# First layer's next-batch convolution as diagonal matmuls on TensorE, and one stash store issued a row later

## The chip, the cores and the metric

The kernel runs on one core of a Trainium2 chip. The metric is device microseconds (us) of one execution, as the median of several runs. PE is TensorE, DVE is VectorE, ACT is ScalarE, POOL is GpSimd, SP is SyncE, which here only issues DMAs.

## The reference, cut to what matters

The program is a stack of four layers over x (4 batches of 512 rows, 512 columns), each an "xattn" block and an "ffn" block. The change touches only the first block of layer 0, a selective state-space block on the context (4 batches of 512 positions, 256 columns, widened to 512 channels, 16 states):

```python
x = jnp.einsum('bld,ed->bel', hidden_states, in_proj_w)
xc = jax.lax.conv_general_dilated(x, conv_w, window_strides=(1,), padding=[(d_conv - 1, 0)],
                                  feature_group_count=d_inner, dimension_numbers=('NCH', 'OIH', 'NCH'))
x = silu(xc + conv_b[None, :, None])
x_dbl = jnp.einsum('bdl,ed->bel', x, x_proj_w)
dt = jax.nn.softplus(jnp.einsum('brl,dr->bdl', dt_low, dt_proj_w) + dt_proj_b[None, :, None])
A = -jnp.exp(A_log)
def step(state, inp):
    d, b, c, u = inp
    state = state * jnp.exp(d[..., None] * A) + (d * u)[..., None] * b[:, None, :]
    return state, jnp.einsum('bdn,bn->bd', state, c)
y = (y + D[None, :, None] * x) * silu(z)
```

The convolution is depthwise: each of the 512 channels has four taps along the sequence. Layer 2 has a block of the same form. Its input projection, convolution, silu and softplus ("the second mixer" below) are also computed inside this first stage, and kept in DRAM for later.

## The kernel before, in words

Channels lie on the 128 partitions in four groups e = 0 to 3, the 512 positions along the free axis; a 128x2048 operand holds all four groups. The first stage (`mamba(0)`) loops over the four batches, and in a batch over the 16 states n. The order of the work on every engine is written out by hand in the `body` of each engine's part; engines meet at semaphores.

In one state, VectorE multiplies (L1850) and scans along the sequence (L1852) all four channel groups. It may start the multiply of state n only when TensorE has turned state n-2 (the last transposes of L1282) and the row of B for state n has come from DRAM (SyncE, L498), and the scan only when ScalarE has made the decay exp(delta*A) (L871, called `decay(n)` and made at ScalarE's place n-2). TensorE transposes the state (L1282, `turn_h`), ScalarE evicts it with a scale (L857, `take_h`), TensorE adds it up, turned back, in PSUM (L1293, `add_h`).

Between these, each engine has other work at fixed places:

- The front of a mixer is: input projection on TensorE (`inproj`), eviction into `m_pad` (ScalarE, L806), convolution (`convolve`, VectorE, L1807 and L1809: 4 multiplies and 12 multiply-adds of 128x512), silu (ScalarE, L813), x projection (TensorE, L1239), dt projection (TensorE; L839 and L840 evict it on ScalarE), `exp_abs` (ScalarE, L846), `softplus` (VectorE, L1821, L1822, L1825), `ln_w` (ScalarE, L850).
- Mixer 1, the second mixer for this batch, runs its convolution after VectorE's state 2, its dt in states 3 and 4, `exp_abs` at the end of ScalarE's place 5, and `softplus` after VectorE's state 6.
- Mixer 0 of the next batch has its input projection in TensorE's state 2, its convolution on VectorE after state 6 (ahead of mixer 1's softplus), silu in ScalarE's place 6, x projection in TensorE's state 6, dt in 7 and 8, softplus after VectorE's state 10. The last batch has none of it.
- Twelve units of keys and values for a later stage (`keys_values`, 16 instructions of 128x256 on TensorE, two evictions at L881, two stores and a weight load issued by GpSimd) stand in the states that `KV_ORDER` lists; the last batch has the first eight.
- PSUM banks 4 to 7 rotate over all tiles in the order of `mamba_tiles`: a tile waits until the tile four before it is evicted (`free`).
- SyncE issues in order. Around state 9: row 8, the store of D*u (1 MB, L511, which waits for ScalarE's L931 of place 7), row 9, a small store, row 10, a load of the context (L501, which waits for the eighth unit of keys and values, made in TensorE's state 9), row 11.

ScalarE's tables: Silu, Exp and Ln need different ones here, and an ACT_TABLE_LOAD stands wherever the next function needs another one; Copy, Abs and Relu run between them without one.

Of the kernel before, what the change touches and what calls it, by code (L numbers as in the profile page):

```python
# [14 lines left out]
P = 128  # L15
# [24 lines left out]
KV_ORDER = (4, 5, 6, 6, 7, 8, 8, 9, 10, 11, 12, 13)  # L40
# [10 lines left out]
def mamba_tiles(last):  # L51
# [4 lines left out]
    for n in range(DS):  # L56
# [15 lines left out]
        if n == 6 and not last:  # L72
            names += [("x", 0)]
        if n in (7, 8) and not last:
            names += [("dt", 0, 2 * (n - 7) + e) for e in range(2)]
# [59 lines left out]
def flamingo(nc, x_d, ctx_d, small_d, rows_d, min_d, mdt_d, ffn_d, qk_d, head_d, wo_d, bit_d, out_d, stages=STAGES):  # L135
    with ExitStack() as stack:
# [83 lines left out]
        pad3 = t3(m_pad, NE)  # L220

# [233 lines left out]
        def _(sp):  # L455
# [10 lines left out]
            for b in range(B):  # L466
                if b == 3:
                    at, n = ROWS["b1"]
                    sp.dma_start(p_b1, rows_d[:, at:at + n].partition_broadcast(P)).then_inc(b1_raw, 16)
# [8 lines left out]
            def mamba(stage):  # L478
# [13 lines left out]
                def body(b, last):  # L492
                    tile = batch_tiles(b, last)
                    for n in range(DS):
# [9 lines left out]
                        if n == 5:  # L504
                            store_bc(1, b, tile("x", 1)[0])
                        if n == 9 and not last:
                            store_bc(0, b + 1, tile("x", 0)[0])
                        if n == 8:
# [155 lines left out]
        def _(pool):  # L664
# [80 lines left out]

            for i in range(KV_LEAD):
# [23 lines left out]
        def _(act):  # L770
# [25 lines left out]
            def mamba(stage):  # L796
# [3 lines left out]
                def take_inproj(m, f, tile):  # L800
                    if not (isinstance(f, int) and f == 0):
                        act.wait_ge(conv_done, 2 * f)
                    for e in range(NE):
                        i, bank = tile("in", m, e)
                        act.wait_ge(tile_filled, i + 1)
                        nc.scalar.activation(pad3[:, e, DC - 1:], ps[:, bank, :], ACT.Copy).then_inc(tile_taken, 1)  # L806

# [75 lines left out]
                def body(b, last):  # L883
                    front_b, front_a = 2 * b + 1, 2 * b + 2
                    tile = batch_tiles(b, last)
                    for n in range(DS):
# [9 lines left out]
                        if n == 8 and not last:  # L896
                            act.wait_ge(sp_corrected, front_b + 1)
                        if n in (8, 9) and not last:
                            take_dt(0, n - 8, tile)
# [21 lines left out]
                        if n == 6 and not last:  # L921
                            silu_u(front_a, 0)
                        if late is not None:
                            take_kv(late, b * (KV_HEADS * 16) + (KV_LEAD + late) * 16, tile)
                        if n == 6:
                            ln_w(front_b)
                            if not last:
                                take_xd(front_a, 0, b + 1, tile)
# [5 lines left out]
                        if n == 9 and not last:  # L934
                            exp_abs(0, tile)
                        if n == 10:
                            if not last:
                                ln_w(front_a)
# [260 lines left out]
        def _(pe):  # L1199
# [16 lines left out]
            def mamba(stage):  # L1216
# [24 lines left out]

                def turn_c(tile):
# [54 lines left out]
                def body(b, last):  # L1297
                    tile = batch_tiles(b, last)
                    for n in range(DS):
# [30 lines left out]
                        if n == 6 and not last:  # L1330
                            xproj(2 * b + 2, 0, tile)
                        if n in (7, 8) and not last:
                            dt(0, n - 7, tile)
# [20 lines left out]
                pe.wait_ge(diag_ready, 1)  # L1354
                batches(pe, body)
# [347 lines left out]
        def _(dve):  # L1703
# [93 lines left out]
            def mamba(stage):  # L1797
# [56 lines left out]
                def body(b, last):  # L1854
                    front_b, front_a = 2 * b + 1, 2 * b + 2
                    tile = batch_tiles(b, last)
                    for n in range(2, DS):
# [9 lines left out]
                        if n == 6:  # L1867
                            if not last:
# [546 lines left out]
```

## Time and profile before

| | |
|---|---|
| median of 3 runs | 3713.45 us (3708.44 to 3716.21) |
| the profiled execution | 3708.7 us, its span 3707.1 us |
| busy share over the span | PE 93%, DVE 81%, ACT 47%, POOL 17% |
| busy share of DVE, first stage (0 to 735 us) | 651.39 of 735 us |
| busy share of PE, first stage | 615.25 of 735 us |
| granted PE clock, mean | 0.966 |

The first stage is the first 730 us. One batch in it is 170.7 us long, from one state 2 to the next. A row of the timeline gives start, duration, engine, line, what is written and read, and how many instructions were merged into the row; in brackets the idle time before it and who ended it. The line numbers are those of the kernel before.

### The profile page before, as it was taken

Reading aid. Unit: us, or ns where it says so; the run is one execution under the profiler, and the core shown is the slowest. Engines: PE = TensorE matmul, PEld = TensorE weight load, DVE = VectorE, ACT = ScalarE, POOL = GpSimd, SP = SyncE. Lnnn points to the kernel's source line nnn. Section 1 sums busy time; section 2 is a strip of 40 time slices with the busy share of each in tenths; the row PEclk is TensorE's granted clock in tenths of the full one; section 3 lists DMA queues with packets and bytes.
Section 4 is the critical chain, followed back from the end, with each engine's and each line's share of the span. In section 5 each row is a group of like instructions: output and inputs, shape, how many; then the busy total and the mean of one; then the engine's idle time right before and its main releaser. Section 6 shows DMA issues by size and latency. Waiting matters only on the chain.

```text
span 3707.1 us, 40267 instructions
## 1 busy us (share of the span) xinstructions
PE 3437.8 (93%) x12305; PEld 1947.9 (53%) x12322; DVE 3013.5 (81%) x4951; ACT 1759.9 (47%) x2748; POOL 623.9 (17%) x596
## 2 busy tenths in 40 slices
PE   7888888799999999899999899999999999999887
PEld 4667676544444444444445788655455455455443
DVE  8899998797979798789889867688388388388797
ACT  6878787633333223334443311255155155155297
POOL 2324251243433220134331000000000000000000
PEclk9899988999999999999999999999999999999998
DMA  4324241524342322443444300221021022021000
GB/s 156 133 65 148 66 147 59 196 86 147 102 153 93 137 84 92 156 153 97 149 156 175 145 24 23 104 70 60 31 70 60 21 70 70 20 70 64 32 12 34
DMA packets 91260, 345.73 MB, mean 93 GB/s; under 512 B 11841, under 2 KB 20161, under 8 KB 77793
## 3 DMA queue, kind: packets, MB, share of 16 engines
q1 hardware_dynamic: 61552, 226.90, 17.4%
q0 software_dynamic: 29552, 116.94, 9.6%
q8 instruction: 76, 1.25, 0.1%
q14 instruction: 80, 0.65, 0.1%
HBM read 280.88 MB, written 62.91 MB: 93 GB/s over the span
## 4 chain that ended last, share of the span: by engine, by line
PE 48%; DVE 27%; issue 14%; ACT 6%; DMA 3%; DVEq 0%; POOL 0%; ACTq 0%; POOLq 0%; SPq 0%
PE ps L1213 30%; PE ps L1610 6%; PE ps L1600 3%; DVE room L1782 3%; PE ps L1441 2%; DVE room L1786 2%; DMA room<-bc_scratch 2%; DVE room L1790 2%; PE ps L1493 2%; PE ps L1282 2%; DVE room L1852 1%; DVE room L1795 1%; DVE room L1850 1%; ACT room L871 1%; DVE room L2320 1%
## 5 line engine op out<-in xcount | busy, mean ns | idle before, releaser
L1213 PE MATMUL ps<-lnT,room 128*128 128x512 f32 x2240 | 987.0, 596 | 23.1 <-DVE room L2007 16.0
L1213 PEld LDWEIGHTS ps<-lnT,room 128*128 128x128 f32 x2240 | 426.0, 191 | 567.9 <-issue 525.5
L1213 PE MATMUL ps<-room 128*128 128x512 f32 (+2 forms) x1807 | 666.8, 524 | 49.6 <-ACT room L1138 21.1
L680 POOL TENSOR_TENSOR idle<-idle 128x1 f32<-128x1 f32 x268 | 447.1, 1668 | 1263.4 <-ACT room L881 434.6
L1213 PEld LDWEIGHTS ps<-room 128*128 128x128 f32 (+1 forms) x1824 | 289.9, 163 | 404.5 <-issue 258.4
L1441 PE MATMUL ps<-room 128*128 128x512 f32 x864 | 379.7, 597 | 8.5 <-DVE room L1961 8.5
L792 ACT ACTIVATE room<-room,small 128x511 f32<-128x511 f32 x256 | 163.6, 710 | 380.6 <-DVE room L1786 380.5
L1852 DVE TENSOR_TENSOR_SCAN room<-room 128x2048 f32<-128x2048 f32 x64 | 283.2, 4425 | 19.0 <-ACT room L871 13.8
L1786 DVE TENSOR_TENSOR_SCAN room<-room 128x2048 f32<-128x2048 f32 x64 | 283.4, 4428 | 5.9 <-DVE room L1782 0.9
L1441 PEld LDWEIGHTS ps<-room 128*128 128x128 f32 x864 | 165.1, 192 | 215.2 <-issue 208.3
L1112 ACT ACTIVATE room<-ps,stat 128x512 f32<-128x512 f32 x256 | 199.0, 777 | 137.3 <-DVE stat L2268 137.3
L1282 PE MATMUL ps<-ident,room 128*128 128x128 f32 x1088 | 164.9, 310 | 86.1 <-DVE room L1852 47.0
L1610 PE MATMUL ps<-room 128*128 128x512 f32 x512 | 242.2, 597 | 0.0
L1768 DVE SCALAR_TENSOR_TENSOR xres<-ps,gates,xres 128x512 f32<-128x512 f32 (+1 forms) x64 | 45.7, 747 | 234.8 <-PE ps L1213 179.9
L2267 DVE TENSOR_REDUCE stat<-ps 128x1 f32<-128x512 f32 x256 | 177.0, 691 | 67.4 <-PE ps L1213 67.1
L1282 PEld LDWEIGHTS ps<-ident,room 128*128 128x128 f32 x1088 | 142.1, 160 | 116.6 <-DVE room L1852 50.3
L1213 PE MATMUL ps<-x,w 128*128 128x512 f32 x768 | 180.2, 395 | 9.2 <-DVE mw L2073 8.2
L1782 DVE TENSOR_TENSOR room<-room 128x2048 f32<-128x2048 f32 x64 | 146.3, 2286 | 40.4 <-DMA room<-bc_scratch 38.7
L857 ACT ACTIVATE room<-ps,room 128x512 f32<-128x512 f32 x256 | 157.1, 699 | 27.8 <-PE ps L1282 27.1
L1213 PEld LDWEIGHTS ps<-x,w 128*128 128x128 f32 x768 | 145.5, 190 | 42.3 <-DVE mw L2073 9.4
L871 ACT ACTIVATE room<-room,small 128x511 f32<-128x511 f32 x256 | 164.5, 739 | 0.5 <-DVE room L1831 0.3
L1850 DVE TENSOR_TENSOR room<-room 128x2048 f32<-128x2048 f32 x64 | 145.8, 2278 | 19.6 <-DMA room<-bc_scratch 18.4
(284 smaller groups left out, 5105.1 us busy)
## 6 DMA issues: line engine op xcount, KB each, us to landing
room<-in_ffn SPq DMA_DIRECT2D x16, 2048.0 KB, 10.9
room<-bc_scratch POOLq DMA_DIRECT2D x128, 256.0 KB, 3.6
room<-kv_stash SPq DMA_DIRECT2D x64, 512.0 KB, 3.4
kv_stash<-room POOLq DMA_DIRECT2D x96, 256.0 KB, 2.4
room<-stash POOLq DMA_DIRECT2D x24, 1024.0 KB, 5.2
room<-in_ffn SPq DMA_DIRECT2D x20, 1024.0 KB, 5.1
room<-in_ffn SPq DMA_DIRECT2D x24, 768.0 KB, 5.6
room<-in_ffn SPq DMA_DIRECT2D x12, 1536.0 KB, 7.3
```

What stands on the lines that cost most here:

```text
L680: nc.gpsimd.tensor_tensor(idle[:, :], idle[:, :], idle[:, :], ALU.add).then_inc(zeros_added, 1)
L871: last_a = nc.scalar.activation(t3(m_dA[n % 2], NE)[:, e, 1:], delta3[:, e, 1:], ACT.Exp, scale=alog[:, e, n:n + 1])
L1112: nc.scalar.activation(P3[:, t, :], ps[:, 4 + t, :], ACT.Exp, bias=nb[:, t:t + 1], scale=rs[:, t:t + 1], accum_out=total[:, t:t + 1]).then ...
L1213: last = nc.tensor.matmul(out, lhsT, rhs, start=(i == 0), stop=(i == len(parts) - 1))
L1282: mm = nc.tensor.transpose(ps[:, bank, e * P:(e + 1) * P], a3[:, e, t * P:(t + 1) * P], ident[:, :])
L1441: mm = nc.tensor.matmul(ps[:, t, :], hT[:, j, t * P:(t + 1) * P], w[:, j, :], start=(g == 0 and j == 0), stop=(g == 3 and j == n - 1))
L1610: mm = nc.tensor.matmul(ps[:, 0, :], kv[:, k, HD:2 * HD], PT3[:, k, :], start=(k == 0), stop=(k == NT - 1))
L1782: v.tensor_tensor(h3, t3(s_du, NE), Bn, ALU.mult).then_inc(s_dBu_ready, 1)
L1786: v.tensor_tensor_scan(s_h, s_dA, s_h, 0.0, ALU.mult, ALU.add).then_inc(s_scan_done, 1)
L1850: link(v.tensor_tensor(t3(h, NE), t3(m_du, NE), Bn, ALU.mult))
L1852: v.tensor_tensor_scan(h, m_dA[n % 2], h, 0.0, ALU.mult, ALU.add).then_inc(scan_done, 1)
L2267: link(v.tensor_reduce(mx[:, t:t + 1], ps[:, 4 + t, :], AX.X, ALU.max, negate=True))
```

## The change

1. `KV_ORDER` becomes (1, 4, 5, 6, 7, 8, 8, ...): one of the two units of state 6 goes, and all that precede it move up, so that the first stands in state 1.
2. Mixer 0's convolution for the next batch is no longer on VectorE. GpSimd makes 16 diagonal matrices (4 taps by 4 groups, 128x128) once, at the start, in the place in `xres` of the last batch's x. In states 3, 4, 5 and 6 TensorE convolves one group each as four matmuls with the shifted `m_pad`, into a rotating PSUM tile. ScalarE takes the tile with Silu and bias (`silu_conv`) at its places 4 to 7, ahead of the state's `take_h`. After the odd groups TensorE waits for its own tile.
3. What follows moves one state on: x projection to state 7, dt to 8 and 9, evictions of dt to ScalarE's places 9 and 10, softplus to VectorE's state 11, `ln_w` to place 11.
4. SyncE issues the store of D*u behind row 9 and the small store instead of ahead of row 9. It waits for x's last batch no longer at the start: that load is issued in the last batch's state 1.

The first batch's own convolution, before the loop, and all of mixer 1's stay on VectorE.

```diff
-KV_ORDER = (4, 5, 6, 6, 7, 8, 8, 9, 10, 11, 12, 13)
+KV_ORDER = (1, 4, 5, 6, 7, 8, 8, 9, 10, 11, 12, 13)
...
+        if n in (3, 4, 5, 6) and not last:
+            names += [("conv", n - 3)]
...
+        m_taps = xres[:, (B - 1) * NT * D:].rearrange("p (j e n) -> p j e n", j=DC, e=NE)
...
                         if n == 9 and not last:
                             store_bc(0, b + 1, tile("x", 0)[0])
-                        if n == 8:
+                        if n == 9:
+
                             place = stashed(2, b)
                             sp.wait_ge(Du_ready, b + 1)
                             sp.dma_start(place, m_z).then_inc(Du_stored, 16)
...
+            for j in range(DC):
+                for e in range(NE):
+                    ins = nc.gpsimd.tensor_scalar(m_taps[:, j, e, :], ident[:, :], t3(const(("cw", 0)), NE)[:, e, j:j + 1], None,
+                                                  ALU.mult)
+                ins.then_inc(taps_ready, 1)
...
+                def silu_conv(f, e, tile):
+
+                    u3, cb = t3(m_next[0][0], NE), const(("cb", 0))
+                    i, bank = tile("conv", e)
+                    act.wait_ge(tile_filled, i + 1)
+                    ins = nc.scalar.activation(u3[:, e, :], ps[:, bank, :], ACT.Silu, bias=cb[:, e:e + 1])
+                    ins.then_inc(tile_taken, 1)
...
+                def convolve(e, tile):
+                    pe.wait_ge(tile_taken, tile("in", 0, e)[0] + 1)
+                    i, bank = tile("conv", e)
+                    free(i)
+                    mm = product(ps[:, bank, :], [(m_taps[:, j, e, :], pad3[:, e, j:j + S]) for j in range(DC)])
+                    mm.then_inc(tile_filled, 1)
+                    if e % 2:
+                        pe.wait_ge(tile_filled, i + 1)
+                        pe.sem_inc(conv_done, 1)
...
                         if n == 6:
-                            if not last:
-                                dve.wait_ge(Du_summed, b + 1)
-                                convolve(front_a, 0, tile)
                             softplus(front_b, 1)
...
-                        if n == 10 and not last:
+                        if n == 11 and not last:
                             softplus(front_a, 0)
```

VectorE behind state 6, before: the end of the convolution (L1809) and then mixer 1's softplus (L1821 to L1825).

```order
L1807 TENSOR_SCALAR room<-room,small 128x512
L427 REGISTER_ALU
L1809 SCALAR_TENSOR_TENSOR room<-room,small 128x512 x2
...
L1820 ISA
L1821 TENSOR_SCALAR room<-room 128x2048
L427 REGISTER_ALU
L1822 SCALAR_TENSOR_TENSOR room<-room 128x2048
```

The same place now: the scan of state 6 (L1898) and the softplus (L1867 on) right behind it.

```order
L1896 TENSOR_TENSOR room<-room 128x2048
L432 REGISTER_ALU
L1897 REGISTER_ALU
L1898 SCALAR_TENSOR_TENSOR room<-room 128x2048
L1866 ISA
L1867 TENSOR_SCALAR room<-room 128x2048
```

All 16 instructions of the convolution are gone from between the two. ScalarE's place 5, before: from the last eviction of dt (L840) to `exp_abs` (L846).

```order
L840 ACTIVATE room<-ps,small 128x512
L856 REGISTER_ALU
L857 ACTIVATE room<-ps,room 128x512 [waits tile_filled]
...
L871 ACTIVATE room<-room,small 128x511 x4
L879 REGISTER_ALU
L880 REGISTER_ALU [waits kv_stored0]
L881 ACTIVATE room<-ps 128x512 [waits tile_filled]
L880 REGISTER_ALU [waits kv_stored1]
L881 ACTIVATE room<-ps 128x512 [waits tile_filled]
L846 ACTIVATE room<-room 128x2048 [waits tile_taken]
```

The same place now (L871 evicts dt, L833 is the new Silu, L888 `take_h`, L902 the decay, L912 keys and values, L877 `exp_abs`).

```order
L871 ACTIVATE room<-ps,small 128x512
L832 REGISTER_ALU
L833 ACT_TABLE_LOAD
L833 ACTIVATE room<-ps,small 128x512 [waits tile_filled]
L887 REGISTER_ALU [waits tile_taken]
L888 ACTIVATE room<-ps,room 128x512 [waits tile_filled]
...
L902 ACT_TABLE_LOAD
L902 ACTIVATE room<-room,small 128x511 x4
...
L877 ACTIVATE room<-room 128x2048 [waits tile_taken]
```

A Silu and two table loads now stand ahead of `exp_abs` in place 5, and the same three in place 4. SyncE from row 9 to row 11, before (L498 the rows, L511 the store of D*u, L501 the context).

```order
L511 ISA [waits Du_ready]
L511 DMA stash<-room 128x2048
L497 REGISTER_ALU
L498 ISA [waits scan_done]
L498 DMA room<-bc_scratch 128x512
L482 REGISTER_ALU
L483 ISA [waits tile_taken]
L483 DMA bc_scratch<-room 32x512
```

The same place now (L509 the rows, L525 the store, L512 the context).

```order
L509 DMA room<-bc_scratch 128x512
L493 REGISTER_ALU
L494 ISA [waits tile_taken]
L494 DMA bc_scratch<-room 32x512
L525 ISA [waits Du_ready]
L525 DMA stash<-room 128x2048
...
L512 ISA [waits tile_filled]
L512 DMA room<-in_ctx 128x1024
L508 REGISTER_ALU
L509 ISA [waits scan_done]
L509 DMA room<-bc_scratch 128x512
```

The store stands behind row 9 now; the load of the context still stands ahead of row 11.

## Rows read from the trace of the kernel before

**Rows 1.** Busy time by stretch: each engine (instructions), granted clock, DMA share, GB/s.

```profile
230.00:401.00 171.00, 147.93 (x798) 114.24 (x798) 158.21 (x103) 134.58 (x210) 57.09 (x60) 0.91 0.32 105
```

**Rows 2.** VectorE's timeline, second batch: start, us, engine, line, what, [idle before].

```profile
231.35 2.28 DVE L1850 TENSOR_TENSOR room<-room 128x2048 f32<-128x2048 f32 x1
...
278.34 0.86 DVE L1807 TENSOR_SCALAR room<-room,small 128x512 f32<-128x512 f32 x2
...
288.60 1.22 DVE L1821 TENSOR_SCALAR room<-room 128x2048 f32<-128x2048 f32 x1
...
294.39 2.28 DVE L1850 TENSOR_TENSOR room<-room 128x2048 f32<-128x2048 f32 x1
...
319.91 2.29 DVE L1850 TENSOR_TENSOR room<-room 128x2048 f32<-128x2048 f32 x1 [4.69 <-DMA room<-bc_scratch]
...
339.75 1.23 DVE L1821 TENSOR_SCALAR room<-room 128x2048 f32<-128x2048 f32 x1 [1.75 <-ACT room L846]
...
345.54 2.28 DVE L1850 TENSOR_TENSOR room<-room 128x2048 f32<-128x2048 f32 x1
...
402.09 2.29 DVE L1850 TENSOR_TENSOR room<-room 128x2048 f32<-128x2048 f32 x1
```

**Rows 3.** ScalarE's timeline, second batch.

```profile
285.88 1.98 ACT L846 ACTIVATE room<-room 128x2048 f32<-128x2048 f32 x1
...
292.40 1.17 ACT L881 ACTIVATE room<-ps 128x512 f32<-128x512 f32 x2
293.59 1.28 ACT L813 ACT_TABLE_LOAD   x1
294.89 2.56 ACT L813 ACTIVATE room<-room,small 128x512 f32<-128x512 f32 x4
```

**Rows 4.** VectorE's timeline, last batch, where there is no convolution of mixer 0.

```profile
572.64 2.28 DVE L1850 TENSOR_TENSOR room<-room 128x2048 f32<-128x2048 f32 x1
...
629.48 1.23 DVE L1821 TENSOR_SCALAR room<-room 128x2048 f32<-128x2048 f32 x1 [9.37 <-ACT room L846]
...
635.27 2.29 DVE L1850 TENSOR_TENSOR room<-room 128x2048 f32<-128x2048 f32 x1
...
660.60 2.29 DVE L1850 TENSOR_TENSOR room<-room 128x2048 f32<-128x2048 f32 x1 [4.60 <-DMA room<-bc_scratch]
```

**Rows 5.** TensorE's timeline, second batch; a 128x512 matmul is two of these instructions.

```profile
228.96 3.60 PE L1312 MATMUL ps<-room 128*128 128x512 f32 x8
232.40 1.91 PE L1293 MATMUL ps<-ident,room 128*128 128x128 f32 x16
...
247.19 2.39 PE L1293 MATMUL ps<-ident,room 128*128 128x128 f32 x16 [0.61 <-ACT room L857]
...
268.12 0.66 PE L1282 MATMUL ps<-ident,room 128*128 128x128 f32 x4 [1.42 <-ACT room L840]
269.28 0.98 PE L1282 MATMUL ps<-ident,room 128*128 128x128 f32 x4 [0.50 <-ACT room L840]
...
288.48 3.72 PE L1213 MATMUL ps<-down_rows,room 128*128 128x256 f32 x16 [0.31 <-ACT room L857]
...
325.51 1.98 PE L1213 MATMUL ps<-room,mw 16*128 16x512 f32 x4
...
333.01 4.27 PE L1213 MATMUL ps<-down_rows,room 128*128 128x256 f32 x16
```

**Rows 6.** SyncE's timeline, second batch.

```profile
313.20 0.36 SPq L511 DMA_DIRECT2D stash<-room  x1
313.81 0.33 SPq L498 DMA_DIRECT2D room<-bc_scratch  x1
...
338.05 0.33 SPq L498 DMA_DIRECT2D room<-bc_scratch  x1
```

**Rows 7.** DMA issues of line 498, same stretch.

```profile
DMA to landing us min/median/max: 3.3/3.8/9.1
```

**Rows 8.** GpSimd's timeline, the head.

```profile
18.20 0.35 POOL L680 TENSOR_TENSOR idle<-idle 128x1 f32<-128x1 f32 x1 [16.08 <-issue]
```

More of the change, by code:

```diff
@@ L71, in mamba_tiles @@
             names += [("dt", 1, 2 * (n - 3) + e) for e in range(2)]
-        if n == 6 and not last:
+        if n in (3, 4, 5, 6) and not last:
+            names += [("conv", n - 3)]
+        if n == 7 and not last:
             names += [("x", 0)]
-        if n in (7, 8) and not last:
-            names += [("dt", 0, 2 * (n - 7) + e) for e in range(2)]
+        if n in (8, 9) and not last:
+            names += [("dt", 0, 2 * (n - 8) + e) for e in range(2)]
         if n == 15 and not last:
@@ L895, in body @@
                             take_dt(1, n - 4, tile)
-                        if n == 8 and not last:
+                        if n == 9 and not last:
                             act.wait_ge(sp_corrected, front_b + 1)
-                        if n in (8, 9) and not last:
-                            take_dt(0, n - 8, tile)
+                        if n in (9, 10) and not last:
+                            take_dt(0, n - 9, tile)
+                        if n == 4 and not last:
+                            act.wait_ge(Du_summed, b + 1)
+                        if n in (4, 5, 6, 7) and not last:
+                            silu_conv(front_a, n - 4, tile)
                         if n:
@@ L926, in body @@
                             ln_w(front_b)
-                            if not last:
-                                take_xd(front_a, 0, b + 1, tile)
+                        if n == 7 and not last:
+                            take_xd(front_a, 0, b + 1, tile)
                         if n == 7:
@@ L1329, in body @@
                             dt(1, n - 3, tile)
-                        if n == 6 and not last:
+                        if n in (3, 4, 5, 6) and not last:
+                            convolve(n - 3, tile)
+                        if n == 7 and not last:
                             xproj(2 * b + 2, 0, tile)
-                        if n in (7, 8) and not last:
-                            dt(0, n - 7, tile)
+                        if n in (8, 9) and not last:
+                            dt(0, n - 8, tile)
                         if n == 15 and not last:
@@ L1879, in body @@
                             v.tensor_tensor(m_u2, m_nd2, m_u2, ALU.mult).then_inc(stash_ready, 1)
-                        if n == 10 and not last:
+                        if n == 11 and not last:
                             softplus(front_a, 0)
```

34 lines of the change are left out of this document (22 added, 12 removed).

## The prediction

> **What bounds the kernel now.** I read the busy time by stretch first. In a middle batch of the first stage VectorE is busy 158.21 of 171 us, TensorE 147.93, ScalarE 134.58 [rows 1]. So VectorE sets the pace by share, with about 13 us idle, but TensorE has only 23 us of room. A share does not tell what follows when work leaves VectorE, so I then read VectorE's timeline for the places where it waits and what ends the wait, then the other engines' timelines for who is nearly late there. A batch is 402.09 - 231.35 = 170.74 us [rows 2].
>
> The decisive pair of rows: mixer 1's softplus starts on VectorE at 288.60 [rows 2], and what it waits for, `exp_abs` on ScalarE, ran from 285.88 to 287.86 [rows 3]. Its input came 0.7 us before VectorE asked. The convolution that the change removes is what VectorE did meanwhile.
>
> **The convolution taken from VectorE.** From 278.34 to 288.60 it costs 10.26 us in each of three batches [rows 2], 30.8 us in all. Without it VectorE asks for the softplus at 278.34 and waits for ScalarE until 287.9, 9.5 us: 0.7 us of the 10.26 is left if nothing else moves. The trace has this case already. The last batch has no such convolution, and there VectorE waits 9.37 us for L846; from state 2 to state 7 it takes 635.27 - 572.64 = 62.63 us [rows 4] against 294.39 - 231.35 = 63.04 us with the convolution [rows 2].
>
> **What makes `exp_abs` later.** It stands at the end of ScalarE's place 5, so it follows TensorE's transposes of state 5, and these follow all TensorE work of states 1 to 4.
> - A matmul with a diagonal of the same shape exists (D*u): 4 of them are 8 instructions, from 228.96 to 232.40, 3.44 us [rows 5]. The new convolution puts 3.44 us into each of states 3 to 6.
> - State 3's 3.44 us stands in front of transposes that before waited 1.42 + 0.50 us for the evictions of dt [rows 5]. Those evictions now run beside it: 1.5 us is added. State 4's: 3.2 us, the waits there being short.
> - The unit of keys and values moved into state 1 is 16 instructions in 3.6 us (3.72 with the overlap of the last) [rows 5]. The 0.61 us wait in state 2 [rows 5] goes, and so does some 0.8 us by which ScalarE lagged there (an estimate): 2.1 us is left.
> - Together 6.8 us on TensorE. On ScalarE, two Silus (2.56/4 = 0.64 us each) and four table loads stand in places 4 and 5: 1.28 + 4 x 1.3 = 6.5 us [rows 3]. Beside TensorE's 6.8 us of delay they mostly fit. If only ScalarE's counted, the delay were about 3.5; if both came in series, about 10.3. I take 6.2, near TensorE's, since a Silu's load runs while its tile is made.
>
> So `exp_abs` ends at 287.9 + 6.2 = 294.1, the softplus starts 5.5 us later than before, and state 7 as well. The 10.26 us come back as a wait of about 15.7.
>
> A page of the Trainium skill would make this worse. In these rows a switch of tables costs 1.3 us: an eviction ends at 293.57, the load starts at 293.59, the Silu at 294.89 [rows 3]. "ScalarE: Activation LUTs", What ACT_TABLE_LOAD costs, gives about 1.28 us for the load and a drain of about 1.38 us besides. By that rule the four switches would put 5.5 us more ahead of `exp_abs` in a batch, some 16 us in all; the trace agrees with the load and shows no such drain, so I leave it out.
>
> **The store behind row 9.** VectorE waits 4.69 us for row 9 [rows 2], because SyncE sat in front of the store until D*u was ready at 313.20, and only then issued the row, at 313.81 [rows 6]. With the store behind it, row 9 goes out at the end of state 7's scan and lands (3.8 us) within the layernorm. This gives 4.69 us per batch and 4.60 in the last [rows 4]. State 9 stands at 5.5 - 4.7 = +0.8 us.
>
> **Row 11, a new wait.** Before, mixer 0's softplus stood behind state 10 and took, with its 1.75 us wait, from 338.00 to 345.54 [rows 2]. Row 11 was issued at 338.05 [rows 6], behind the load of the context, which waits for a unit of keys and values of TensorE's state 9 (from 333.01) [rows 5]. The softplus covered its 3.8 us flight [rows 7]. Now the softplus stands behind state 11, so VectorE wants row 11 at 338.0 + 0.8 = 338.8, while TensorE is late. Its balance up to that unit: 6.8, + 3.44 in state 5, + 3.44 - 3.6 - 3.44 in state 6 (one unit and the x projection gone, which is 8 instructions as a convolution is), + 3.44 - 1.98 in state 7 (dt gone to 8) [rows 5], about 8.1; some waits of TensorE in states 7 to 9 (4 to 5 us) absorb half. I take 4.3, bounds 2.5 and 8. Row 11 is issued at 342.4 and lands at 346.1: a wait of 7.3 us, and state 11 starts 0.5 us later than before. Then come its 6.75 us and the softplus with its wait, 7.5 us, which before lay ahead of it: state 12 and all later ones are +8. Since ScalarE's `exp_abs` of mixer 0 may run partly ahead, I take +7.3 a batch. TensorE's mean granted clock is 0.91 of the full 2.4 GHz in such a batch [rows 1]; I count no gain from denser work.
>
> **At no cost.** GpSimd's diagonals: 16 small operations at the start, where it was idle for 16.08 us ahead of its first store's 18.20 [rows 8]; with one 1 MB load fewer in the head against them, -2 to +4 us. The last x load: 1 MB in the last batch, needed at its state 8. TensorE's wait for its own tile: 0.3 us, inside the sums.
>
> **The sum.** Three batches at +7.3 = +21.9. The last batch: -4.6 for row 9, +2.1 because the moved unit delays its `exp_abs` too: -2.5. Head 0. So +19.4 us on the profiled execution's 3708.7 us (its span 3707.1 and 1.6 around it): 3728. The median of the runs is 4.8 us above that execution, which would give 3733; I say 3730. By bounds: with 3.5 us for `exp_abs` and row 11 hardly late, a batch is 0 and the total -3 to 0, 3706; with 10.3 and 8, a batch is +12, the total +34, and about 3750.
>
> **The rivals.**
> - Faster, "VectorE is the bound": all 10.26 and 4.69 us come off, 30.8 + 18.7 = 49 us, 3664. For it: VectorE's 93% share of a batch [rows 1]. Against it: the 9.37 us wait in the last batch. It needs `exp_abs` 9 us earlier, and nothing moves it up.
> - Slightly faster, "the wait takes the convolution's place exactly, the store pays": TensorE's and ScalarE's additions hide, row 11 comes in time. A batch is -0.7 - 4.7 = -5.4, total about -21, 3692. Against it: TensorE's waits ahead of state 5's transposes are 0.61, 1.42 and 0.50 us [rows 5], less than the 6.9 us of new matmuls there. It decides this way if `exp_abs` moves by less than 1 us.
> - No change: `exp_abs` moves by about 3.5 us and row 11 is late by 2 or 3: within 7 us of before.
> - Much slower, ScalarE in series: TensorE waits for ScalarE's evictions behind each new load, as rotating banks make it. +12 a batch, 3750. Counted in the order, ScalarE gets 7 more loads a batch (15 for 8), 9 us on 134.58 busy [rows 1].
> - That the convolution is not moved: excluded by the order of instructions.
>
> **How the numbers follow.** My forecast (+8 to +30 us) has 0.6, much slower 0.13, no change 0.14, slightly faster 0.09, fully faster 0.04. A measurement tells about 0.2% (7.4 us) from no change. So slower 0.74, same 0.14, faster 0.12. The range from 3700 to 3752 leaves out the fast rivals and the far end of the slow one, 2 in 10 at most.
>
> **What would show it.** Right: in a middle batch, VectorE waits 14 to 17 us for `exp_abs` behind state 6, row 9 without a wait, row 11 with 5 to 8 us, a batch of 176 to 180 us; the last batch 2 to 3 us shorter. Wrong at the first step: `exp_abs` within 1 us of 56.5 us after state 2's start. Wrong at row 11: no wait there, then the batch is near 171. The forecast fails as a whole if a batch is below 170 us.

## The result, and the profile after

| | before | after |
|---|---|---|
| median (shared chip) | 3712.81 us (3708.44 to 3716.21, 4 runs) | 3743.48 us (3740.68 to 3745.26, 4 runs) |
| profiled execution | 3708.7 us | 3742.7 us |
| middle batches of the first stage | 170.7, 170.6 us | 182.2, 184.0 us |
| last x row of the first stage starts at | 724.33 us | 755.51 us |

The ratio is 1.0083, 95% interval 1.0065 to 1.0100: slower, by 31 us. Of the 34 us between the profiled executions, 31.2 are there at the end of the first stage. Counted from state 2 to state 2 they are: head -0.2, the three batches with a convolution for the next one +9.9, +11.4 and +13.5, the last -2.0, its end -1.4. An offset below is the time since the start of a batch's state 2.

In the second batch VectorE is now busy 148.40 of 182.15 us, ScalarE 142.62, TensorE 158.61 [rows 1] at a higher granted clock (0.94 for 0.91). VectorE did lose its 10 us of work; the batch got 11 us longer.

```profile
241.07:423.22 182.15, 158.61 (x829) 117.28 (x828) 148.40 (x88) 142.62 (x215) 57.64 (x60) 0.94 0.31 99
```

VectorE's timeline of that batch, changed kernel (L1896 and L1898 are a state's multiply and scan, L1853 the convolution's first multiply, L1867 the softplus; state 2 starts at 241.07):

```profile
241.07 2.28 DVE L1896 TENSOR_TENSOR room<-room 128x2048 f32<-128x2048 f32 x1
...
249.89 0.49 DVE L1853 TENSOR_SCALAR room<-room,small 128x512 f32<-128x512 f32 x1 [1.23 <-ACT room L826]
...
275.58 2.29 DVE L1896 TENSOR_TENSOR room<-room 128x2048 f32<-128x2048 f32 x1 [2.23 <-PE ps L1325]
280.59 4.42 DVE L1898 TENSOR_TENSOR_SCAN room<-room 128x2048 f32<-128x2048 f32 x1 [2.72 <-ACT room L902]
...
291.06 4.42 DVE L1898 TENSOR_TENSOR_SCAN room<-room 128x2048 f32<-128x2048 f32 x1 [3.08 <-ACT room L902]
306.64 1.36 DVE L1867 TENSOR_SCALAR room<-room 128x2048 f32<-128x2048 f32 x1 [11.15 <-ACT room L877]
...
312.57 2.29 DVE L1896 TENSOR_TENSOR room<-room 128x2048 f32<-128x2048 f32 x1
...
333.24 2.28 DVE L1896 TENSOR_TENSOR room<-room 128x2048 f32<-128x2048 f32 x1
...
359.63 2.29 DVE L1896 TENSOR_TENSOR room<-room 128x2048 f32<-128x2048 f32 x1 [8.21 <-DMA room<-bc_scratch]
...
367.61 1.23 DVE L1867 TENSOR_SCALAR room<-room 128x2048 f32<-128x2048 f32 x1 [1.14 <-ACT room L877]
...
373.40 2.28 DVE L1896 TENSOR_TENSOR room<-room 128x2048 f32<-128x2048 f32 x1
```

State 12 of the kernel before, which [rows 2] leave out:

```profile
352.29 2.27 DVE L1850 TENSOR_TENSOR room<-room 128x2048 f32<-128x2048 f32 x1
```

Against it and [rows 2], as offsets: softplus of mixer 1 at 65.6 for 57.3 (it waits 11.15 us), state 7 at 71.5 for 63.0, state 9 at 92.2 for 88.6 and without a wait, state 11 at 118.6 for 114.2, behind a new wait of 8.21 us for its row, state 12 at 132.3 for 120.9.

ScalarE's timeline (L833 is the Silu out of the convolution's bank, L877 `exp_abs`, L912 the eviction of keys and values), then SyncE's (L525 the store of D*u, L512 the context, L509 rows):

```profile
294.48 1.28 ACT L833 ACT_TABLE_LOAD   x1
296.53 0.69 ACT L833 ACTIVATE room<-ps,small 128x512 f32<-128x512 f32 x1 [0.77 <-PE ps L1246]
...
304.71 1.90 ACT L877 ACTIVATE room<-room 128x2048 f32<-128x2048 f32 x1
...
344.69 0.60 ACT L912 ACTIVATE room<-ps 128x512 f32<-128x512 f32 x1 [4.39 <-DMA kv_stash<-room]
347.12 0.60 ACT L912 ACTIVATE room<-ps 128x512 f32<-128x512 f32 x1 [1.84 <-DMA kv_stash<-room]
```

```profile
334.77 0.35 SPq L525 DMA_DIRECT2D stash<-room  x1
...
354.98 0.35 SPq L512 DMA_DIRECT2D room<-in_ctx  x1
355.59 0.33 SPq L509 DMA_DIRECT2D room<-bc_scratch  x1
```

`exp_abs` starts 63.6 us after state 2, for 54.5 before [rows 3]. Row 11 is issued at 114.5, for 106.7 [rows 6].

### The profile page after: what moved, and what is told of

The parts are those of the page before. It is cut to its first block, busy times and chain, and to the rows that moved or that the text cites. A ratio compares the mean times of both kernels' runs of the same rounds, so it can differ in the third digit from the quotient of the medians.

```text
span 3741.0 us, 40462 instructions
## 1 busy us (share of the span) xinstructions
PE 3469.7 (93%) x12401; PEld 1954.1 (52%) x12418; DVE 2985.1 (80%) x4903; ACT 1786.5 (48%) x2769; POOL 655.8 (18%) x612
## 4 chain that ended last, share of the span: by engine, by line
PE 51%; DVE 25%; issue 13%; ACT 7%; DMA 3%; POOL 0%; DVEq 0%; ACTq 0%; POOLq 0%; SPq 0%
PE ps L1246 32%; PE ps L1656 5%; PE ps L1487 3%; PE ps L1646 3%; DVE room L1828 2%; DMA room<-bc_scratch 2%; PE ps L1539 2%; PE ps L1325 2%; DVE room L1832 2%; DVE room L1836 1%; DVE room L1898 1%; DVE room L1896 1%; ACT room L902 1%; ACT room L888 1%; PE ps L1336 1%
## 5 line engine op out<-in xcount | busy, mean ns | idle before, releaser
L1246 PE MATMUL ps<-lnT,room 128*128 128x512 f32 x2240 | 989.0, 598 | 25.3 <-DVE room L2052 18.7
L694 POOL TENSOR_TENSOR idle<-idle 128x1 f32<-128x1 f32 x268 | 466.4, 1740 | 1264.1 <-ACT room L912 463.1
L1898 DVE TENSOR_TENSOR_SCAN room<-room 128x2048 f32<-128x2048 f32 x64 | 283.2, 4425 | 29.5 <-ACT room L902 24.1
L2312 DVE TENSOR_REDUCE stat<-ps 128x1 f32<-128x512 f32 x256 | 176.9, 691 | 67.1 <-PE ps L1246 66.8
L1325 PE MATMUL ps<-ident,room 128*128 128x128 f32 x1088 | 154.4, 298 | 79.6 <-DVE room L1898 38.6
L1325 PEld LDWEIGHTS ps<-ident,room 128*128 128x128 f32 x1088 | 134.0, 154 | 112.9 <-DVE room L1898 44.6
L1896 DVE TENSOR_TENSOR room<-room 128x2048 f32<-128x2048 f32 x64 | 145.9, 2280 | 37.9 <-DMA room<-bc_scratch 27.2
L888 ACT ACTIVATE room<-ps,room 128x512 f32<-128x512 f32 x256 | 155.9, 693 | 25.0 <-PE ps L1325 24.3
L902 ACT ACTIVATE room<-room,small 128x511 f32<-128x511 f32 x256 | 164.0, 728 | 0.6 <-DVE room L1877 0.3
## 6 DMA issues: line engine op xcount, KB each, us to landing
room<-in_ffn SPq DMA_DIRECT2D x16, 2048.0 KB, 10.8
```

Source lines behind the costliest of these rows:

```text
L694: nc.gpsimd.tensor_tensor(idle[:, :], idle[:, :], idle[:, :], ALU.add).then_inc(zeros_added, 1)
L888: nc.scalar.activation(hT3[:, t, :], ps[:, bank, :], ACT.Copy, scale=cT3[:, t, column:column + 1]).then_inc(tile_taken, 1)
L902: last_a = nc.scalar.activation(t3(m_dA[n % 2], NE)[:, e, 1:], delta3[:, e, 1:], ACT.Exp, scale=alog[:, e, n:n + 1])
L1246: last = nc.tensor.matmul(out, lhsT, rhs, start=(i == 0), stop=(i == len(parts) - 1))
L1325: mm = nc.tensor.transpose(ps[:, bank, e * P:(e + 1) * P], a3[:, e, t * P:(t + 1) * P], ident[:, :])
L1896: link(v.tensor_tensor(t3(h, NE), t3(m_du, NE), Bn, ALU.mult))
```

## The experiments

Every row but "after" (the result's four runs) is timed in five rounds against the kernel before on the same chip (its medians there: 3711.2, 3710.8 and 3709.7 us). "Batches" are the two middle ones, "stage" the start of the last x row, both from VectorE's timeline of the profiled execution. That is one execution, and executions of one kernel lie up to 21 us apart (3700.5 to 3721.3 for the kernel before), so a few us between two stages tell little by themselves.

| kernel | median us | ratio to before, 95% | batches | stage |
|---|---|---|---|---|
| before | 3711.2 | 1 | 170.7, 170.6 | 724.3 |
| b_store: + store behind row 9 | 3702.7 | 0.9975 (0.9962 to 0.9988) | 167.5, 169.4 | 710.3 |
| b_kv: + new order of keys and values | 3717.5 | 1.0012 (1.0000 to 1.0025) | 177.4, 176.9 | 736.2 |
| b_conv: + convolution on TensorE | 3768.5 | 1.0156 (1.0135 to 1.0178) | 191.9, 191.3 | 783.8 |
| after: all three | 3743.5 | 1.0083 (1.0065 to 1.0100) | 182.2, 184.0 | 755.5 |
| a_store8: after, without the store's move | 3748.3 | 1.0096 (1.0078 to 1.0115) | 184.3, 186.4 | 763.4 |
| a_oldkv: after, without the new order | 3753.7 | 1.0110 (1.0092 to 1.0127) | 188.9, 187.3 | 771.2 |
| a_kctx: after, context's load in place 13 | 3761.1 | 1.0134 (1.0114 to 1.0154) | 189.4, 187.8 | 775.0 |
| a_kctx11: the same, behind row 11 | 3748.4 | 1.0098 (1.0080 to 1.0115) | 183.7, 184.6 | 759.0 |
| a_tap1: after, one tap of four | 3743.5 | 1.0085 (1.0067 to 1.0104) | 183.5, 178.6 | 751.6 |
| a_copy: after, Relu for Silu | 3726.6 | 1.0043 (1.0027 to 1.0059) | 177.2, 179.6 | 744.0 |
| a_group: after, Silus together | 3738.2 | 1.0078 (1.0059 to 1.0098) | 182.6, 182.3 | 755.3 |
| b_late0: b_store, softplus and context's load one place later | 3706.0 | 0.9990 (0.9979 to 1.0001) | 173.8, 173.1 | 726.2 |
| b_both: b_late0, last batch's softplus behind state 7 | 3712.5 | 1.0005 (0.9992 to 1.0018) | 173.7, 174.0 | 728.2 |

**The parts alone.** The store:

```diff
-                        if n == 8:
+                        if n == 9:
                             place = stashed(2, b)
```

> The kernel before with one edit: the store of D*u stands behind row 9 on SyncE instead of ahead of it (place 9 for place 8). Theory A (what sets a batch is the way over TensorE and ScalarE, VectorE's waits are partly a shadow of it): VectorE's wait of 4.69 us for row 9 goes, of which about two thirds stay as a gain at the batch's end, since TensorE and ScalarE are then nearer to late in states 9 to 13: 4 x 3 = 12 us, about 3701. Theory B (the prediction's own term, each wait counted where it stands): 3 x 4.69 + 4.60 = 18.7 us, about 3694. Theory C (the store pays nothing, the wait comes back at the next state): 3713.

Row 9's wait is gone, and the kernel is 8.5 us faster by the medians (14 us at the stage's end of the profiled execution, which lies 10.8 us under this kernel's median). Neither sum is the 18.7 us of waits removed: some came back one place later, at mixer 0's softplus, 4.23 us for 1.75 [rows 2]. Theory A is the nearest.

```profile
310.21 2.28 DVE L1850 TENSOR_TENSOR room<-room 128x2048 f32<-128x2048 f32 x1
...
332.53 1.35 DVE L1821 TENSOR_SCALAR room<-room 128x2048 f32<-128x2048 f32 x1 [4.23 <-ACT room L846]
```

The order of keys and values:

```diff
-KV_ORDER = (4, 5, 6, 6, 7, 8, 8, 9, 10, 11, 12, 13)
+KV_ORDER = (1, 4, 5, 6, 7, 8, 8, 9, 10, 11, 12, 13)
```

> The kernel before with one edit: the new order of the units of keys and values (one moved from state 6 to state 1). Theory A: 16 instructions of 3.6 us stand ahead of state 5's transposes, so mixer 1's exp_abs is about 2 us later; before, it was ready 0.7 us ahead of VectorE behind the convolution, so 1.4 us in each of three batches and 2.1 in the last come through: +6, about 3719. Theory B (the unit fills time in which TensorE waited anyway): within 2 us of 3713. Theory C (exp_abs is later by the full 3.6 us): 3 x 2.9 + 3.6 = +12, about 3725.

The median says +6.3, as theory A did. The middle batches are 6.3 to 6.7 us longer, and the place is another than A's: VectorE waits 4.2 us for the first evictions of the input projection ahead of mixer 1's convolution, where before there was no wait. The moved unit does not stand ahead of those projections; an idle stretch of TensorE does, told at the end. Without it they would be 2.5 and 1.9 us longer, and `exp_abs`, 6.6 us later in the second batch, is 2.4 later beyond it. The first batch has no such stretch ahead of it: `exp_abs` is 1.1 us later there, and the batch is as long as before (171.78 for 171.77). So most of this run's time is the idle stretch and not theory A's term, and A's number came out by luck.

The convolution alone is the changed kernel with both other edits undone:

> The third part of the change alone: the kernel before with the convolution on TensorE in states 3 to 6 and what moves with it, but with the old order of keys and values and the store of D*u ahead of row 9. Theory I (parts add as each measured in the changed kernel: the store gives back about 5 us there, the new order of keys and values about 10): about 3759. Theory J (parts add as each measured in the kernel before: store -8.5, order of keys and values +6, so the convolution is the change's +31 less these): +33, about 3744. Theory K (the prediction's sum for the convolution alone, its row 11 and exp_abs terms without store and without the moved unit): about +30, 3741.

It costs 59 us, more than any theory had. A middle batch is 21 us longer, and 13 of these are a longer wait for row 9. VectorE's, ScalarE's and SyncE's timelines of its third batch (state 2 at 443.82; L854 is the eviction of the x projection, L964 is D*u):

```profile
551.26 2.29 DVE L1896 TENSOR_TENSOR room<-room 128x2048 f32<-128x2048 f32 x1 [17.70 <-DMA room<-bc_scratch]
```

```profile
522.02 0.60 ACT L912 ACTIVATE room<-ps 128x512 f32<-128x512 f32 x1 [6.02 <-DMA kv_stash<-room]
524.27 0.60 ACT L912 ACTIVATE room<-ps 128x512 f32<-128x512 f32 x1 [1.65 <-DMA kv_stash<-room]
...
541.28 0.59 ACT L854 ACTIVATE room<-ps 48x512 f32<-48x512 f32 x1 [3.76 <-PE ps L1272]
541.78 2.55 ACT L964 ACTIVATE room<-room,small 128x512 f32<-128x512 f32 x4
```

```profile
544.50 0.36 SPq L525 DMA_DIRECT2D stash<-room  x1
545.12 0.33 SPq L509 DMA_DIRECT2D room<-bc_scratch  x1
```

Row 9 stands behind the store, the store behind ScalarE's D*u, and that behind two units of keys and values in state 6: the second unit's eviction waits 6.0 us until GpSimd's store of the first has left its buffer. D*u's store goes out 100.7 us after state 2, for 81.9 before [rows 6]. Some 7 of these 19 us belong to the second unit: with one unit in state 6, in the changed kernel, the store goes out at 93.7 (334.77 above). The rest is `exp_abs`, itself late, and the eviction of the x projection, which now stands ahead of D*u and waits 3.76 us for TensorE.

A good part of the 6.0 us is not the store. Ahead of each store GpSimd runs a tiny addition on a tile of its own (L694), and the store is issued only when that is done. GpSimd's timeline, then VectorE's beside it:

```profile
504.74 0.19 POOL L694 TENSOR_TENSOR idle<-idle 128x1 f32<-128x1 f32 x1 [7.26 <-ACT room L912]
...
515.68 3.96 POOL L694 TENSOR_TENSOR idle<-idle 128x1 f32<-128x1 f32 x1 [8.48 <-ACT room L912]
519.58 0.56 POOL L703 DMA_DIRECT2D kv_stash<-room  x1
```

```profile
515.23 4.42 DVE L1898 TENSOR_TENSOR_SCAN room<-room 128x2048 f32<-128x2048 f32 x1
```

At 504.74 VectorE stood idle, waiting for `exp_abs`, and the addition took 0.19 us. At 515.68 it ran beside a scan, took 3.96 us, and ended with the scan (519.64 and 519.65). The eviction started 2.4 us after the store's issue. No run takes this addition away.

So the change's two smaller parts repair what its first part does, and each is worth more beside the convolution than in the kernel before: the store's move 15 us (b_conv to a_oldkv), the new order 20 us (b_conv to a_store8), together 25.

**The parts taken back from the changed kernel.**

> The changed kernel with one edit: the store of D*u stands ahead of row 9 again. Theory A: row 9 is late by about 5 us again and most of it comes through, +3 to +5 us per batch and in the last: +14, about 3757; row 11's wait gets shorter by what state 9 starts later. Theory B (the store's move gives its full 4.69 us four times): +19, about 3762. Theory C (in the changed kernel VectorE would only wait at row 11 instead, whose row depends on TensorE and not on VectorE): row 11's wait falls from 8 to 4 us, the time stays within 4 us of 3743.

Between A and C: 4.8 us. VectorE waits 8.23 us for row 9 again, and row 11's wait falls from 8.21 to 1.53 us. One wait stands for the other.

> The changed kernel with the old order of the units of keys and values (state 1 has none, state 6 has two). In the kernel before, the new order alone cost 12 us up to the end of the stage, 4.2 us of it in each batch as VectorE's wait for the input projection ahead of mixer 1's convolution. Theory A (the way TensorE to ScalarE sets the batch): that wait (1.6 to 3.5 us here) goes and state 7 starts 2 to 4 us earlier, but the unit now stands in state 6 in front of mixer 0's exp_abs, and some of it is paid there: -5, about 3739. Theory B (the parts of the change add up): -6 to -12, about 3735. Theory D (TensorE alone is the bound, and its idle time in state 1 is lost): 3.6 us more per batch, +11, about 3754.

Theory D's number, 3754, but not shown for its reason: as in b_conv, the second unit of state 6 waits for GpSimd's store of the first (7.04 us in the second batch, 3.82 of them GpSimd's addition beside a scan).

**Row 11.**

```diff
-                        if n == 10 and not last:
+                        if n == 13 and not last:
                             sp.wait_ge(tile_filled, tile("kv", KV_OWN - 1, 1)[0] + 1)
```

> The changed kernel with one edit: SyncE's load of the context, which stood ahead of row 11 (place 10) and waits for a unit of keys and values, is issued in place 13. Theory B (the prediction's own term: row 11's wait of 7.3 us, measured 8.2 to 10.2, adds to the path because the row sits behind this load): that wait goes and comes off in three batches, 3 x 8 = 24 to 27 us, about 3718. Theory A (TensorE and ScalarE are what is late there): row 11 comes in time, but VectorE then waits some 7 to 8 us more for mixer 0's exp_abs behind state 11 (it waited 0.3 to 1.1 us there): within 4 us of 3743.

Row 11's wait went, and the time rose by 18 us. The 1 MB store of state 11, no longer behind the context's load, went out at 349.24, 103.9 us after state 2 for 115.1 in the changed kernel. A store of keys and values, issued beside it at 349.06, landed late: ScalarE waited 4.91 us for it (1.84 in the changed kernel):

```profile
349.24 0.36 SPq L529 DMA_DIRECT2D stash<-room  x1
```

```profile
354.60 0.60 ACT L912 ACTIVATE room<-ps 128x512 f32<-128x512 f32 x1 [4.91 <-DMA kv_stash<-room]
```

So the load was put behind row 11 but ahead of that store (`n == 11`):

> The changed kernel with the context's load on SyncE right behind row 11 instead of ahead of it, and still ahead of the 1 MB store of state 11 (with the load in place 13, that store went out 6.9 us earlier, a store of keys and values landed later, and the time was 17 us longer). Theory A (TensorE to ScalarE set the batch, row 11 is a shadow): row 11 in time, but the wait for mixer 0's exp_abs takes its place: within 4 us of 3743. Theory B (row 11's wait of 8.2 to 10.2 us is on the path): -24, about 3719. Theory H (an earlier state 11 brings VectorE's waits and the 1 MB store forward and costs as in the run with place 13): about 3760.

Row 11 is now in time, and nothing is won (+5 us by the medians, with overlapping intervals). VectorE's timeline, state 11 and behind it:

```profile
352.55 2.27 DVE L1896 TENSOR_TENSOR room<-room 128x2048 f32<-128x2048 f32 x1
356.01 4.42 DVE L1898 TENSOR_TENSOR_SCAN room<-room 128x2048 f32<-128x2048 f32 x1 [1.20 <-ACT room L902]
370.96 1.23 DVE L1867 TENSOR_SCALAR room<-room 128x2048 f32<-128x2048 f32 x1 [10.53 <-ACT room L877]
```

The 8.21 us at row 11 have become 10.53 at the softplus. Theory B, the prediction's own term as a cause, is dead: the wait was real, but taking it away only moves it. The run also fits the reading of a_kctx: with the 1 MB store back behind the load, ScalarE's wait is 1.81 us again.

**TensorE or ScalarE.** One tap (three of the four are left out):

```diff
-[(m_taps[:, j, e, :], pad3[:, e, j:j + S]) for j in range(DC)]
+[(m_taps[:, j, e, :], pad3[:, e, j:j + S]) for j in range(1)]
```

> The changed kernel, but each tile of the convolution on TensorE is made of one tap of four (three taps are left out, so it computes something else): 2 matmul instructions for 8, some 2.6 us less in each of states 3 to 6, 10.3 us a batch; ScalarE's work and all loads of tables stay. Theory A (TensorE's added matmuls delay exp_abs): exp_abs of mixer 1 comes about 4 us earlier (63.6 to about 59 us after state 2), that of mixer 0 about 7 us earlier: -7 in each of three batches, -21, about 3722. Theory E (ScalarE's Silus and table loads are what delays it): within 4 us of 3743. Theory F (both the TensorE term and the wait at row 11): -10 per batch, about 3713.

Some 10 us a batch less of matmuls at full clock change nothing in the median (the profiled execution is 7 us shorter, the batches differ by 5 us from each other). Theory A, that TensorE's added matmuls are what costs, fell here as far as this run can tell. In TensorE's timeline the room became waits for ScalarE, and after them a unit of keys and values ran at 6.00 us for 3.72 [rows 5]:

```profile
283.70 1.11 PE L1325 MATMUL ps<-ident,room 128*128 128x128 f32 x4 [1.34 <-ACT room L833]
284.61 6.00 PE L1246 MATMUL ps<-down_rows,room 128*128 128x256 f32 x16
...
309.16 0.66 PE L1325 MATMUL ps<-ident,room 128*128 128x128 f32 x4 [2.73 <-ACT room L833]
```

The granted clock is 0.60 in those 6.00 us, for 1.00 in the same unit of the changed kernel. Over the whole batch it is 0.91 for 0.94, and TensorE is busy only 2.0 us less than in the changed kernel (156.65 for 158.61), not 10:

```profile
239.88:423.35 183.47, 156.65 (x811) 118.39 (x810) 148.45 (x88) 143.35 (x217) 57.23 (x60) 0.91 0.29 98
```

So in this batch the run tests less than its edit promises: most of what was left out came back as slower matmuls. The first batch is the cleaner test. There TensorE is busy 7.0 us less (148.28 for 155.23), yet `exp_abs` comes no earlier (62.4 for 62.0) and the batch is 1.2 us shorter (180.47 for 181.66). The third batch has no idle stretch of TensorE ahead of it, as it has in the changed kernel (told at the end); beyond that it is 2.0 us shorter, with TensorE busy 13.4 us less (148.82 for 162.24).

Then the tables, `ACT.Relu` for `ACT.Silu` at L833 (the convolved branch gets another function):

> The changed kernel with Relu for Silu behind the convolution on TensorE (it computes another function): the Silus of states 4 to 7 then need no other table, some 7 loads of tables of 1.29 us go in a batch, 4 of them ahead of mixer 1's exp_abs; TensorE's work stays. Theory A: they lie mostly beside TensorE's matmuls: exp_abs about 1 to 2 us earlier, -2 to -3 a batch, about 3736. Theory E (they are in series): exp_abs 5.2 us earlier, the sum over a batch -7 to -9, about 3720. Theory G (fully beside TensorE): within 3 us of 3743.

17 us of the 31 went by the medians, with seven loads a batch (8 for 15), some 9 us of ScalarE. `exp_abs` came 2.3 and 4.0 us earlier in the two middle batches, 2.5 if the idle stretch told at the end is taken out of both kernels. Theory A said 7 us, theory E 23. The three batches with the convolution are 6.2, 5.0 and 4.4 us shorter, 15.6 in all, but the last one, which has neither convolution nor Silu of this kind, is 4 us longer up to its last x row. At the stage's end 11.5 us are left (744.0 for 755.5); the other 5 us of the 17 come behind the stage, in work that the edit does not touch. ScalarE's timeline (state 2 at 235.00) now shows waits for TensorE where a load stood:

```profile
277.05 0.69 ACT L833 ACTIVATE room<-ps,small 128x512 f32<-128x512 f32 x1
...
289.54 0.69 ACT L833 ACTIVATE room<-ps,small 128x512 f32<-128x512 f32 x1 [2.07 <-PE ps L1246]
...
296.27 1.93 ACT L877 ACTIVATE room<-room 128x2048 f32<-128x2048 f32 x1
```

To keep the function and lose the loads, the tiles were copied out and the Silus run together at place 7:

```diff
-ins = nc.scalar.activation(u3[:, e, :], ps[:, bank, :], ACT.Silu, bias=cb[:, e:e + 1])
...
+nc.scalar.activation(u3[:, e, :], ps[:, bank, :], ACT.Copy).then_inc(tile_taken, 1)
+if e == NE - 1:
...
+    for k in range(NE):
+        ins = nc.scalar.activation(u3[:, k, :], u3[:, k, :], ACT.Silu, bias=cb[:, k:k + 1])
```

> The changed kernel, but each tile of the convolution is taken out of its bank by a Copy, and the four Silus run one behind the other in place 7: two loads of tables for eight, 4 more evictions of 0.6 us. With Relu for Silu (7 loads less a batch) the time was 17 us shorter, and mixer 1's exp_abs came 2.3 to 4 us earlier. Theory L (ScalarE's table loads in front of its evictions are what the convolution on TensorE costs): exp_abs of mixer 1 as with Relu, at 61.4 us after state 2, mixer 0's softplus 1 to 3 us later than with Relu: 10 to 14 us shorter than the changed kernel, about 3731. Theory M (each ScalarE instruction is in series, loads or not): 6 loads x 1.29 - 4 x 0.6 = 5.3 us a batch, -16, about 3728. Theory A (TensorE's matmuls are what counts; already spoken against by the run with one tap): within 4 us of 3743.

`exp_abs` came even a little earlier than L said (61.0 and 60.9), but only 5 us were won by the median and none at the stage's end. The four Silus and two loads stand in one piece ahead of the x projection, and VectorE's wait at row 11 rose to 11.16 us. Mixer 0's `exp_abs` starts at 125.0 and 124.7, for 119.6 and 122.0 with Relu: what was saved ahead of mixer 1's was paid ahead of mixer 0's.

**A better version.** On top of b_store, mixer 0's softplus behind state 11 and the context's load behind row 11:

> The kernel before with the store behind row 9 (3703 by itself) and two moves more: mixer 0's softplus behind state 11 on VectorE, and the context's load behind row 11 on SyncE. With the store alone VectorE waits 4.2 to 5.1 us for mixer 0's exp_abs behind state 10. Theory N: state 11's 6.75 us stand in that wait, row 11 is issued in time (ahead of the context's load): the wait goes, -4 a batch in three, about 3691. Theory O (ScalarE and TensorE set the pace in states 9 to 13 here as in the changed kernel, where the context's load moved in this way gave nothing): the wait comes back behind state 11 or in state 12: within 4 us of 3703.

Theory O, 3.3 us above b_store by the medians: no wait at the softplus, but 6.89 us at state 13's scan, whose decay stands on ScalarE behind an eviction that waits 5.03 us for a store of keys and values.

```profile
365.54 4.42 DVE L1852 TENSOR_TENSOR_SCAN room<-room 128x2048 f32<-128x2048 f32 x1 [6.89 <-ACT room L871]
```

> As the run before it (store behind row 9, mixer 0's softplus behind state 11, context's load behind row 11), and in the last batch alone mixer 1's softplus stands behind state 7, its Ln on ScalarE behind D*u. In the last batch VectorE waits 8.0 to 9.4 us for mixer 1's exp_abs behind state 6. Theory P: state 7's 6.7 us stand in that wait, the last batch is 5 to 6.5 us shorter than in the run before it. Theory Q (TensorE's transposes and ScalarE's decays for states 8 and 9 then are late, as state 7 comes earlier): 0 to 2 us.

Theory Q, and worse: the last batch, from its state 2 to its last x row, is 151.1 us for 146.0. VectorE waits 7.00 us at state 11 of that batch, behind TensorE's transposes. That `ln_w`, now later on ScalarE, is the reason is not shown: TensorE also sits idle for 3.40 us at 640.68, waiting for nothing that the profile shows, and ScalarE waits 6.01 us for a store of keys and values. b_store has the lowest median, 3702.7 us; its interval overlaps that of b_late0.

## Why the prediction was right in its sign and 13 us short, point by point

- **VectorE is not the bound.** Right: 10.26 us of work left it and were replaced by waits. The wait at the softplus was 11.15 us, not the 14 to 17 that were to show the forecast right; the waits ahead of it grew by 5.6 us beside the idle stretch (2.23, 0.67 and 2.65 more at states 5 and 6).
- **`exp_abs`, +6.2 us.** Nearly right for what I summed: in the first batch it starts 62.0 us after state 2 for 55.1, +6.8. In the second it is +9.1, of which 1.7 us were there at state 3 already (the idle stretch of TensorE, no part of my sum). But a_copy shows that my split was off: ScalarE's loads ahead of it cost some 2.5 us and were not hidden beside TensorE, and over a batch the loads cost 4.4 to 6.2 us. a_tap1's first batch shows the other side: without three quarters of the added matmuls `exp_abs` came no earlier. The moved unit of keys and values, put at 2.1 us, delayed it by 1.1 us in b_kv's first batch. So the sum is near and its terms are not, which is partly luck. I had named "ScalarE in series" a rival at +12 a batch and 3750 us, with a chance of 0.13; the batches came out at +9.9 to +13.5, and 3743 is nearer to that rival than to my 3730.
- **The store, -4.7 us per batch.** The wait went and state 9 came at +3.6 (+0.8 predicted). As a gain it was mis-sized: 4.8 us in the changed kernel and 8.5 in the kernel before, not 18.7.
- **Row 11, a new wait of 7.3 us.** The row shows it: 8.21, and 10.2 and 8.7 in the batches beside it. The step failed as a cause: a_kctx11 takes the wait away and gains nothing. What is late there is mixer 0's `exp_abs`, at 124.5 for 106.5, though the edit moved it by one place only. My +7.3 a batch hangs on this row, so that it came within 3 us of the first batch's +9.9 is luck.
- **Not seen: TensorE's idle stretch at the loop's back edge.** The first batch has none ahead of it and is +9.9. In the next two, state 3 comes 1.7 and 3.5 us later than the 17.0 of before, and 9.9 + 1.7 and 9.9 + 3.5 are their +11.4 and +13.5. That is 5 of the 12 us by which the stage's end missed my sum (31.2 against 19.4).
- **Mis-sized: +9.9 for +7.3 in a batch without it**, 8 us in three. ScalarE's waits for stores of keys and values at this place (4.39 and 1.84 us above) are no explanation: the kernel before has them too.

```profile
324.60 0.60 ACT L881 ACTIVATE room<-ps 128x512 f32<-128x512 f32 x1 [3.57 <-DMA kv_stash<-room]
329.14 0.60 ACT L881 ACTIVATE room<-ps 128x512 f32<-128x512 f32 x1 [3.94 <-DMA kv_stash<-room]
```

- **Last batch, -2.5, and head, 0.** The numbers are right: -2.0 to its y multiply and -0.2. The terms of the last batch are not, so this is partly luck: `exp_abs` is 0.2 us later, not 2.1, state 9 comes the full 4.7 us earlier, and 3 of these are gone again by state 14 (124.4 for 126.2).

What stays open: why seven loads, 9 us of ScalarE in each of three batches, were worth 15.6 us over these and not 27; what the rest of the change's 31 us is beside the loads' 11 to 17, since neither the added matmuls (a_tap1, with its clock) nor row 11 (a_kctx11) give it back; and b_conv's 59 us beyond its row 9.

## What to carry to other kernels

When work moves from the busiest engine to another, follow the two engines that hand tiles to each other through few banks, and price what is added to each by taking it away: here 9 us of table loads a batch gave back 4.4 to 6.2, and 10 us of matmuls gave back nothing in the median. Read the granted clock in such a run: the engine that was given room may run slower. A wait seen in a trace is priced in the same way, not by its length; here one of 8 us in three batches was worth nothing and four of 4.7 were worth 8.5. Before two units of work are put into one state, look at who empties their shared buffer. The hidden third party was a store of keys and values: issued late in b_conv and a_oldkv, as GpSimd's addition ahead of it ran beside a scan of VectorE, and slow to land in a_kctx. In b_late0 both are there, and no run separates them.

## What the runs showed of the hardware

TensorE sits idle for 2 to 3 us where the loop over the batches turns back, in the changed kernel and in no case in the kernel before ([rows 5], 228.96 follows without a gap). Over all kernels the stretch lasts 1.5 to 3.1 us. TensorE's first matmuls then take 5.39 us in one of the two cases of the changed kernel, for 3.60, at a granted clock of 0.69; so they do in 5 of the 23 cases of all kernels. TensorE's timeline of the changed kernel:

```profile
240.34 3.69 PE L1355 MATMUL ps<-room 128*128 128x512 f32 x8 [2.92 <-issue]
...
422.55 5.39 PE L1355 MATMUL ps<-room 128*128 128x512 f32 x8 [1.92 <-issue]
```

The page's queues go with it (packets, MB, share). In the changed kernel, in b_late0 and in before:

```profile
q8 instruction: 97, 1.59, 0.2%
```

```profile
q8 instruction: 94, 1.54, 0.2%
```

```profile
q8 instruction: 76, 1.25, 0.1%
```

Over all kernels: 76 packets of 16 KB and no gap (before, b_store), 86 and one gap (a_tap1), 94 to 97 and two gaps (the other eleven). In 20 us around the first gap (225 to 245) three such packets move in the changed kernel and none in before. The Trainium skill ("Runtime: NRT & Kernel Launch", Instruction fetch mechanics) says that code comes in blocks of 16 KiB and that a taken branch out of the window held stalls until its block is fetched. These runs agree in so far as packets of this size and the idle stretch come together; that the fetch is the cause is not shown, and the kernel before takes the same turn without a stretch. What decides whether it happens stays open: b_late0's TensorE program is, instruction for instruction, that of the kernel before, and it has the gaps. In b_late0 it puts the batch's state 3 back by 2.0 and 1.5 us, in b_kv by 4.2 and 4.4.

A GpSimd operation on 128x1 took 0.19 us while VectorE was idle and 3.96 us beside one of its scans, ending with it (the rows of b_conv above; 3.82 us in a_oldkv, and 3.96 us in the kernel before at 322.77, with a scan from 322.32 to 326.74).

GpSimd's 16 multiplies for the diagonals took 11.30 us in the head, which is 0.2 us shorter than before in all.
